# Last layer of a four-layer graph network: GpSimd waits for VectorE's messages ahead of every four gathers

## What is computed

```
h = relu(edge_feat @ W1 + b1)                     # 262144 x 64
w = (h @ W2 + b2).reshape(e, 4, 8, 8)             # four 8x8 matrices for each edge
s_e, v_e = s[src], v[src]                         # rows of x, gathered by source node
m0 = ALPHA * (einsum(s_e*sh0, w_000) + C110 * einsum(v_e, sh1, w_110))
m1 = ALPHA * (einsum(s_e, sh1, w_011) + einsum(v_e*sh0, w_101))
out = segment_sum([m0, m1], dst) + SI_SCALE * (x @ si_w)
```

## Time and profile before

| | |
|---|---|
| time, median of 3 runs | 9348.64 us (9328.12 to 9374.58) |
| the profiled execution, its own time | 9420.17 us |
| its span, first to last instruction | 9418.3 us |
| busy in the span: TensorE, VectorE, ScalarE, GpSimd | 65%, 45%, 32%, 42% |
| mean granted TensorE clock | 0.66 |
| stretch in which VectorE works on chunks 1 to 124 of the last layer | 5333 to 9333 us |

### The profile page before, as it was taken

One profiled execution on the slowest core, in us unless ns is written; L12 is line 12 of the kernel. 1 busy time (PEld: TensorE's weight loads), 2 busy tenths in 40 slices (PEclk: granted clock), 3 DMA queues, 4 the chain that ended last, 5 costly groups with the idle time before them and its releaser, 6 DMA issues.

```text
span 9418.3 us, 117068 instructions
## 1 busy us (share of the span) xinstructions
PE 6121.2 (65%) x38929; PEld 4566.3 (48%) x38930; DVE 4272.7 (45%) x8292; ACT 2973.6 (32%) x7181; POOL 3933.3 (42%) x4168
## 2 busy tenths in 40 slices
PE   6555555555555555556568477777777777777777
PEld 3355555545545454533234355555555555555555
DVE  3344444444444444411011356555555655655656
ACT  3332322333323332300000243443444344344344
POOL 2333344333333334354440444444444444444442
PEclk6666666666666666766668566666666666666666
DMA  8322222333333333377679000000000000000000
GB/s 264 141 100 104 103 101 96 121 118 114 114 114 114 114 114 114 118 261 263 241 234 295 20 17 18 17 17 17 18 17 17 18 17 17 18 17 17 17 19 15
DMA packets 596615, 865.34 MB, mean 92 GB/s; under 512 B 170817, under 2 KB 418690, under 8 KB 579458
## 3 DMA queue, kind: packets, MB, share of 16 engines
q1 hardware_dynamic: 363858, 385.79, 12.9%
q10 hardware_dynamic: 99504, 406.06, 10.8%
q0 software_dynamic: 133120, 71.57, 4.2%
HBM read 455.19 MB, written 406.85 MB: 92 GB/s over the span
## 4 chain that ended last, share of the span: by engine, by line
PE 34%; another core or an unknown queue 26%; issue 20%; DVE 12%; ACT 5%; DMA 2%; ACTq 1%; DVEq 0%; SPq 0%
PE psum L1010 10%; PE psum L962 8%; PE psum L1185 5%; PE psum L1066 4%; PE psum L1176 3%; DVE arena L1840 3%; DVE arena L1826 3%; DVE arena L1818 2%; ACT arena L748 2%; PE psum L1096 1%; DVE q_sum L1833 1%; DMA arena<-adj 1%; DVE arena L1814 1%; PE psum L1033 1%
## 5 line engine op out<-in xcount | busy, mean ns | idle before, releaser
L614 POOL DMA_INDIRECT gathered<-rel_table,idx x2048 | 1932.9, 944 | 2726.3 <-DMA idx<-key_i 2040.5
L614 POOL DMA_INDIRECT gathered<-x_rows,idx x2048 | 1937.7, 946 | 2502.0 <-DMA idx<-in_src 1589.1
L1010 PE MATMUL psum<-arena 64*128 64x128 f32 x8192 | 790.9, 355 | 1389.5 <-ACT arena L748 866.7
L1185 PE MATMUL psum<-w,arena 65*128 65x256 f32 x4096 | 1519.6, 540 | 103.6 <-DVE arena L1818 61.7
L1010 PEld LDWEIGHTS psum<-arena 64*128 64x128 f32 x8192 | 709.2, 257 | 1458.3 <-ACT arena L747 908.9
L747 ACT COPY arena<-psum 128x512 f32<-128x512 f32 x1024 | 602.1, 588 | 2548.1 <-remote 1631.4
L1185 PEld LDWEIGHTS psum<-w,arena 65*128 65x128 f32 x4096 | 1122.2, 281 | 411.4 <-issue 110.0
L962 PE MATMUL psum<-arena 128*128 128x184 f32 x4096 | 985.9, 399 | 158.3 <-issue 154.8
L962 PEld LDWEIGHTS psum<-arena 128*128 128x128 f32 x4096 | 892.4, 247 | 323.5 <-issue 300.5
L1818 DVE TENSOR_TENSOR arena<-psum,arena 128x256 f32<-128x256 f32 x1536 | 704.8, 486 | 314.4 <-ACT arena L862 168.7
L1502 DVE TENSOR_TENSOR arena<-iota,psum 128x2048 f32<-128x2048 f32 x128 | 292.5, 2285 | 1207.2 <-PE psum L1010 945.9
(11 more groups left out here) (217 smaller groups left out, 5638.5 us busy)
## 6 DMA issues: line engine op xcount, KB each, us to landing
adj<-arena ACTq DMA_DIRECT2D x128, 2048.0 KB, 6.4
arena<-adj SPq DMA_DIRECT2D x93, 2048.0 KB
counts<-arena ACTq DMA_DIRECT2D x128, 512.0 KB, 7.3
arena<-counts SPq DMA_DIRECT2D x64, 1024.0 KB, 11.8
arena<-adj SPq DMA_DIRECT2D x40, 1024.0 KB
rel_table<-table_out ACTq DMA_DIRECT2D x32, 1024.0 KB
rel_table<-arena ACTq DMA_DIRECT2D x32, 1024.0 KB
gathered<-rel_table,idx POOLq DMA_INDIRECT x2048
```

Of the source, the lines that this page charges most:

```text
L614: pool.indirect_dma_start(gathered[:, s, j, :], None, rows[l], bass.IndirectOffsetOnAxis(ap=idx[:, s, j:j + 1], axis=0),).then_inc(group_i ...
L1010: mm = pe.matmul(psum[:, 2 * r + a, 2 * HIS * i:2 * HIS * (i + 1)], oh_lo[h][rows_of, u, :], oh_both[h][rows_of, u, :, :].rearrange("p k c ...
L1185: mm = pe.matmul(pair[g % 2][:, WN * q:WN * q + WN], hidden[:, s % 2, q, P * g:P * g + P], w2[:, :], start=True, stop=True)
```

## The change

GpSimd's loop over the last layer is split. The first round (chunks 0 to 3) gathers as before. From chunk 4 on, GpSimd waits ahead of tiles 0, 4, 8 and 12 until `msg_ready` reaches a value that is kept in a register and goes up by one with each group. It starts at 4 (4 - 3) + 2 = 6, which is reached when group 0 of chunk 1 is made: so the four gathers of group g of chunk c wait for the messages of group g of chunk c-3. No other engine's instructions change, and the number of gathers is the same. The path for other inputs (the outer `Else`) is as before.

```diff
+PACE_3 = 3
...
-            def gather_chunk(l, s):
+            def gather_chunk(l, s, pace=None):
 
                 pool.wait_ge(idx_in[s], pool.snap(due[s]))
                 pool.reg_add(due[s], due[s], 16)
                 for j in range(TILES):
+                    if pace is not None:
+                        pace(j)
                     pool.indirect_dma_start(
...
-                gather(3)
+                messages = pool.alloc_register("messages_due")
+                pool.reg_mov(messages, GROUP * (SLOTS - PACE_3) + 2)
+
+                def messages_made(j):
+
+                    if j % GROUP == 0:
+                        pool.wait_ge(msg_ready, pool.snap(messages))
+                        pool.reg_add(messages, messages, 1)
+
+                pool.wait_ge(rows_out[2], 16)
+                for s in range(SLOTS):
+                    gather_chunk(3, s)
+                with looped(pool, 1, ROUNDS):
+                    for s in range(SLOTS):
+                        gather_chunk(3, s, messages_made)
```

## The result

In this first comparison the changed kernel takes **8881.82 us** median of 4 runs (8853.41 to 8896.33) where the kernel before takes 9354.34 us (9328.12 to 9374.58): ratio **0.9493**, 95% interval 0.9458 to 0.9527, 472.5 us saved. The profiled execution has a span of 8894.5 us at a mean clock of 0.682, where the one before had 9418.3 us at 0.66: 523.8 us less. Behind L606 every line number is 17 higher than before, except in the gathers (L614 is now L617): L1805 is L1822, L1811 is L1828, L1818 is L1835, L1843 is L1860.

The account below looks back on a forecast made before the run. VectorE was taken to bound the last layer, waiting on signals late beneath GpSimd's gathers. Going from 32.26 to 27.0 us a chunk over 124 chunks saves 652 us: 9348.64 - 652 = 8697 us, range 8040 to 9350.

Parts of the forecast that it names:

- What bounds the kernel: Last layer: VectorE is on the path at 32.26 us a chunk, 10.0 of them waiting at L1811 for TensorE's product.
- The cost of the wait: GpSimd's added waits, 496 in the last layer: 0 to 2.4 us a chunk, all on GpSimd, off the path.
- The cycle: Last layer after the change: gathers, stall, message group, 5.0n + 3.15 + r us; taken as 27.0 us a chunk, saving 652 us.
- n: Groups of four gathers that GpSimd runs back to back before VectorE gets stuck; expected between 3 and 4.
- r: Time from the last gather's start until VectorE goes on: 2.6 us in one place, 4.2 us in another.
- What is late next: After the change: VectorE's own 19.2 to 21.7 us a chunk and, close to it, GpSimd's 20.0.
- The signs: Last layer: chunk 26 to 28 us, L1811's wait some 5, runs of 12 to 16 gathers, no index or `group_in` waits.
- Rival A: Short pauses between groups of four gathers let every signal through: 22.0 us a chunk, 8077 us; chance 0.28.
- Rival B: Spread gathers delay the TensorE-ScalarE ping-pong, n = 2: 33.1 us a chunk, 9453 us, slower; chance 0.17.
- Rival C: Gathers aren't the cause; TensorE stops at a fixed point of its program: no gain, 9349 us; chance 0.10.
- my reading: In a run of gathers signals pass freely for some 5 to 7 us, then are late until the run is over.

Follow-up runs that it names:

- Mostly: Kernel before, but last layer has the change's wait in rounds 1 to 15 (60 chunks), then other fetch rules: 5699.72 us against 5700.08, ratio 0.9997.
- few4: Kernel before, but in the last layer only one tile of each four is gathered, so output is wrong: 5706.59 us, ratio 1.0004.
- pause: Kernel before plus 28 GpSimd register additions ahead of every fourth last-layer gather, which left no instruction: 5706.37 us; serves as short-chip trace of the kernel before.
- pause_iota: Kernel before plus a GpSimd iota of 128x512 ahead of every four last-layer gathers: 5925.18 us against 5704.21.
- mixed: Kernel before, but last layer runs seven GpSimd rules in turn (as before, iotas, fewer gathers, plain DMAs, waits); 5808.5 us against 5701.5, three repeats 5801.4 to 5805.9.
- once: Changed kernel, but GpSimd waits only once per chunk, then gathers all 16 in one run: 5708.73 us, 20.08 us a chunk.
- spload: Kernel before, but in the last layer SyncE loads fixed rows by plain DMAs in place of all GpSimd gathers: 5702.84 us, 19.99 us a chunk.

## Why the prediction was right, and where it wasn't

The direction and the range held: 8881.8 us lies between 8040 and 9350. The predicted 8697 us is 185 us too low; it had 652 us of gain, and 472.5 came.

**What bounds the kernel.** Right for the long chips. The wait at L1811 was the one to shorten, and it gave 3.1 of the 4.0 us that a chunk lost.

**The cost of the wait.** Right as far as it was measured. I took it to lie on GpSimd alone. Mostly puts a wait that doesn't hold at nothing, with an interval of 0.1%, over 60 chunks in which GpSimd had no slack. Where the wait holds, the gather starts 0.76 us after the end of VectorE's L1860 (all 269 waits of over 1 us in the trace after). That lies on GpSimd too, but in the cycle it is on the path, as the next term shows. On the long chip VectorE never waited for a gathered row.

**The cycle.** The mis-sized term. The forecast was 5.0n + 3.15 + r per cycle, taken between n = 3 and n = 4 as 27.0 us a chunk. The cycle shown above has n = 4 and 28.15 us (7025.90 to 7054.05). By its parts: from first to last gather 20.82 us, where the formula has 20.0 - 1.25 = 18.75; then r = 2.21 us, at which the earlier trace rows had 2.6; then 5.12 us until the next gather, where it has 4.4. So the two missing parts are **2.07 us of pauses inside the run**, 1.82 of it in the one idle stretch of 2.12 us ahead of 7042.97 (where 0.30 is usual), and **0.72 us** between the end of the message group and the gather that it releases. 18.75 + 2.21 + 4.4 = 25.36, and with 2.07 and 0.72 it is 28.15. I had named the pause inside the run (VectorE's uneven groups "leave GpSimd a pause of 2 us") as a reason for a larger n, which it was, and forgot that the pause itself takes time. That the forecast is no further off is in part luck: with the n = 4 and the r of this cycle my formula gives 25.4 us, and choosing a value towards n = 3 made up for over half of what it leaves out. 1.15 us more in 124 chunks, 28.15 against 27.0, is 143 us of gain too much, and the mean of 28.29 makes it 160. Of the other 25 us, 6 are the median of the kernel before, which a fourth run moved up, and 19 the difference between the profiled executions (523.8 us apart, 32 of it outside these chunks) and the medians (472.5). The chunks aren't all alike: of the 124 periods 69 lie between 27 and 29 us, 19 below 23 and 21 above 33 us, where chunks go in pairs of some 22 and 36 us, eight groups in 57 us, that is two runs of 16 gathers. In number of gathers n was 4 in 74 runs, 3 in 23 and 5 in 21.

**What is late next.** I said VectorE's and GpSimd's own 19.2 to 21.7 us. It never came to that on a long chip; on a short one both engines are at 20.0 to 20.1, and one gather of four (few4) leaves it at 20.07, so VectorE is the bound there.

**The signs.** VectorE's chunk at 26 to 28 us: 28.29, just outside. L1811's wait at some 5 us: 7.0, above it by what the forecast is short of. Runs of 12 to 16 gathers with a wait of some 7 us for the message group: 6.41 and 6.38 us in the rows, 6.8 us on average, with 21 runs of 20 gathers above what I said. No wait for indices: so it is. The indicator multiply's own wait shorter: 447.3 to 133.5 us. No wait for `group_in` at L1822: so it is, VectorE's idle time ahead of it is never over 0.8 us.

**Rival A** (short pauses are enough, 22 us a chunk): not what happened. The pause of 2.12 us in the cycle didn't even let through a signal whose matmuls ended in it, at 7042.50: VectorE stood until 7048.93. Whether a regular pause would do better was the question of pause, pause_iota and mixed, and it stays open: the first had no pause, and the others met short chips only. **Rival B** (slower, n = 2): no; n was mostly 4, and ScalarE's wait for the ping-pong at the old L852 didn't grow (899.6 + 378.5 us before, 905.0 + 170.0 + 154.8 after, at L869). What did grow is TensorE's idle time ahead of L1202, 103.6 to 343.6 us in the pages, 296.9 of it for VectorE's L1835: TensorE is two groups ahead there and waits for a free PSUM pair.

**Rival C** (the gathers aren't the cause). On long chips it is refuted by the change itself, twice, at 0.9493 and 0.9489: nothing but the time of the gathers was altered, and VectorE's wait for TensorE and ScalarE's for itself fell. The late rises of `w_made` say the same from the other side: the matmuls were done. But my reading was told as a property of gathers, and that is wrong. The Trainium skill, "SBUF — State Buffer", section "Who interferes with whom", says that "PE and ACT never wait on anyone"; the short chips agree with the rule as I read it, with 0.84 us for a hop beneath gathers and 13.9 us of wait in 124 chunks, and the long chips don't, with 23.75 us and 1245 us. **Two things are needed: gathers, and a chip in a condition that I can't name.** It isn't special to the last layer: before chunk 1 of that layer the long chip is already at 5302 to 5333 us and the short one at 3138 us, and nearly all of that difference lies in layer 0, where gathers run (1.74 times, against 1.12 without them). The stretch without gathers keeps the DMA engines busy for 0.90 and 0.92 of the time, so late signals would show less in it.

**What stays open.** Whether the change helps by tying GpSimd to VectorE at every group, or only by starting the gathers later in the chunk: the runs stayed 16 long, and once, which would tell, met a short chip. What differs between the chips; five of six is also a small number, and whether it is the chip or its state at that hour can't be told from one long chip. One difference is in the traces themselves: the same program leaves 95237 recorded rises of semaphores in pause and 37444 in the kernel before. Every time of the experiments comes with a recorded span, so no run tells whether the recording has a part in the delay. Whether on a long chip signals would also be late beneath plain DMAs from GpSimd, or beneath SyncE's. How long a pause has to be, and how many gathers may be run without one. And why 55 of 141 long waits of the kernel before ended inside a run. The kernels that would tell (few4, spload, once, the mixed ones) met short chips only, and no working pause of the size wanted was tried in a whole layer.

## What to carry to other kernels

An engine that only fetches ahead can be tied to the consumer's progress. With three chunks of lead VectorE never waited for a row on the long chip, though each release took 0.76 us; where the wait never held it cost nothing. When waits are long though the producer has ended and no engine is near full, look at the same code in a place with other traffic around it, and then on another chip, before a mechanism is written down: here the kernel before took 5700 to 5717 us on five chips of six, and where its gathers were traced on those they delayed nothing. And a cycle is summed with every pause in it, those that let another engine catch up too.

## What was not expected of the hardware

- The same kernel takes 5700 to 5717 us on five chips and 9264 us on a sixth (9354 in the first comparison). Busy times of VectorE and GpSimd are the same within 1%. On the long one, while gathers run, semaphores rise late: the hop of 0.80 us at the layer's head takes 24.43 us at worst (ScalarE's copy at 5278.31, the one after the 23.75 us of the earlier trace rows).
- TensorE's granted clock followed the waits: 0.64 at 32 us a chunk, 0.71 at 28, 0.83 at 20, and 0.74 where iotas slowed a short chip to 24.4 us.
- An iota of 128x512 takes 0.57 us on GpSimd with unit step (pause_iota) and 1.63 us with its inner step zero (mixed).
- From the end of the VectorE instruction that signals to the start of the gather that waited for it: 0.76 us, in all 269 waits of over 1 us in the trace after.
- 28 register additions ahead of every fourth gather, whose result nothing reads, left no instruction in the trace (117068 with them and without).
